# Last batch of a cross-attention and FFN kernel: gate and up on all 256 columns, roots split between VectorE and GpSimd

## The chip, the cores and the metric

The kernel runs on one core of one Trainium2 chip. The metric is device time in microseconds of one execution. A core has TensorE (PE in the profile, PEld its weight loads), VectorE (DVE), ScalarE (ACT), GpSimd (POOL) and the queue that issues transfers (SP). They run their own instruction lists and meet only at semaphores.

## The reference

`x` is (8 batches, 256 rows, 256 features), the context (8, 77, 256). All of it is float32; the FFN weights are integers scaled by 1/127.

```python
x = x + xattn(layernorm(x), ctx)         # 16 heads of 64, softmax, w_out, bias, tanh(gate)
x = x + ffn(layernorm(x))

def ffn(x):                              # HIDDEN = 768
    gate = x @ wg.T ; up = x @ wu.T
    h = silu(gate) * up
    return h @ wd.T
```

## The kernel before

After a start-up phase (weights, `t_all`, values) the kernel runs eight rounds, one per batch of 256 rows (two tiles of 128 rows, t = 0 and 1, called a and b in names). A round does the attention of batch b and, filled in between, the FFN of batch b-1. Each engine has its stages in an order written out by hand (`PE_ORDER`, `DVE_ORDER`, `ACT_ORDER`, `POOL_ORDER`). After the last attention there is nothing left to fill in, so the last batch's projection, second layernorm and FFN have orders of their own (`PE_END`, `DVE_END`, `ACT_END`, `POOL_END`): the tail, from about 288 us on. A name such as `O0.7` is stage O0 of round 7.

Float32 products are made from a high part, rounded to float32r, and a low part, the rest: ScalarE makes `_hi`, VectorE or GpSimd subtracts for `_lo`, and TensorE adds the products.

The stages of the tail:
- O0, O1 (lines 883 to 891): output projection of tile a and b, 24 matmuls each. R0, R1 (1315, 1318): the residual sum and its statistics.
- na0 to na11, nb0 to nb11 (1359 to 1382): per tile, aggregation of the statistics, variance plus eps, a seed of the inverse root and three refinements of three steps, each waiting for the one before. la, lb (1386): normalisation into `x1_hat`.
- xa, xb: on TensorE two transposes of `x1_hat` (804), on ScalarE `x2_hi` (1030), on VectorE `x2_lo` (1391). The tile on TensorE goes to banks 0 and 6 of PSUM.
- ga0 to ga5, gb0 to gb5 (844): for each of six slices f of the hidden dimension, eight matmuls of one tile: gate and up, high and low, two halves of the contraction.
- ta, tb (ScalarE, 1035): tanh of the gate. Ha, Hb (VectorE, 1399, 1402): gating and product with up. ha, hb: `h_hi` on ScalarE (1040), `h_lo` on GpSimd (1148).
- D0.7, D1.7 (870, 873): the down projection of batch 6, 12 matmuls each, put between. Y0.7, Y1.7 its results (1307). da, db (855, 857): that of the last batch, 12 matmuls each. ya, yb its results, each followed by a store of the tile (539).

In the other rounds gate and up (825) treat both tiles at once, 256 columns, eight matmuls per f. `hid_of` and `tanh_of` give the last batch a place of its own for each f, so that no slice waits for an earlier one's buffer there.

GpSimd has a routine of its own for inverse roots, used at the start for the first layernorm:

```python
        def rsqrt(step, r, v, half, tmp):
            tt = nc.gpsimd.tensor_tensor
            n = v.shape[1]
            step(tt(half, v, consts[:, 1, 0:n], ALU.mult))
            step(nc.gpsimd.tensor_scalar(r.bitcast(I32), v.bitcast(I32), -0.5, RSQRT_SEED, ALU.mult, ALU.add))
            for _ in range(3):
                step(tt(tmp, r, r, ALU.mult))
                step(tt(tmp, tmp, half, ALU.mult))
                step(tt(tmp, tmp, consts[:, 2, 0:n], ALU.add))
                step(tt(r, tmp, r, ALU.mult))
```

Of the kernel before, what the change touches and what calls it, by code (L numbers as in the profile page):

```python
# [30 lines left out]
P = 128  # L31
# [26 lines left out]
PE_END = "O0.7 O1.7 xa D0.7 ga0 ga1 ga2 ga3 ga4 ga5 xb D1.7 gb0 gb1 gb2 gb3 gb4 gb5 da db".split()  # L58
ACT_END = "xa ta0 ta1 ha0 ta2 ha1 ta3 ha2 ta4 ha3 ta5 xb ha4 tb0 ha5 tb1 hb0 tb2 hb1 tb3 hb2 tb4 hb3 tb5 hb4 hb5".split()
DVE_END = ("R0.7 na0 na1 na2 na3 na4 na5 na6 na7 na8 na9 na10 na11 la R1.7 xa nb0 nb1 nb2 Y0.7 nb3 nb4 Ha0 nb5 nb6 Ha1 nb7 nb8 Ha2 "  # L60
           "nb9 nb10 nb11 lb Ha3 Ha4 xb Ha5 Hb0 Y1.7 Hb1 Hb2 Hb3 Hb4 Hb5 ya yb").split()
POOL_END = "ha0 ha1 ha2 ha3 ha4 ha5 hb0 hb1 hb2 hb3 hb4 hb5".split()
# [16 lines left out]
def xattn_ffn_kernel(nc, x, ctx_in, ln_gamma, ln_beta, w_q, w_kv, w_out, b_out, gate,  # L79
# [26 lines left out]
    X_STEPS = 4 + 12  # L106
    assert HB * K <= BANK and DC == 2 and NT == 2 and 2 * DH == P and RC == VS + 1 and K <= P
# [7 lines left out]
    with whole:  # L115
# [138 lines left out]
        x1_done, stat_done, ln_step, x1hat_done = sem("x1_done"), sem("stat_done"), sem("ln_step"), sem("x1hat_done")  # L254
        aggr_done, spare_cleared = sem("aggr_done"), sem("spare_cleared")
# [133 lines left out]

        def count_in_tile(t, f):  # L390

            return FC * (B - 1) + FC * t + f + 1
# [214 lines left out]
        def _(pe):  # L607
# [221 lines left out]
            def gate_up_tile(t, f, general):  # L829

                if f == 0:
                    pe.wait_ge(x2hi_done, B + t)
                if t == 1:
                    pe.wait_ge(hid_done, count_in_tile(0, f))
                elif LAST_BANKS[f] == bank["D0"]:
# [12 lines left out]
            def down_tile(t, general):  # L848

                if t == 0:  # L850
                    pe.wait_ge(y_done, NT * (B - 1))
                o = ps[:, LAST_DOWN_BANKS[t], 0:D]
                for f in range(FC):
                    pe.wait_ge(hhi_done, count_in_tile(t, f))
                    mm(o, whole(h_hi[:, f, tile(t)], general), whole(wd[:, f, :], general), start=f == 0, stop=False)
                    pe.wait_ge(hlo_done, count_in_tile(t, f))
                    ins = mm(o, whole(h_lo[:, f, tile(t)], general), whole(wd[:, f, :], general), start=False, stop=f == FC - 1)
                ins.then_inc(down_done, 1)
# [34 lines left out]
            def stages_of(general):  # L893
# [11 lines left out]
                for t in range(NT):  # L905
                    stages["x" + "ab"[t]] = ("start", transpose_x1_tile, t)
                    stages["d" + "ab"[t]] = ("start", down_tile, t, general)
                    for f in range(FC):
                        stages["g" + "ab"[t] + str(f)] = ("start", gate_up_tile, t, f, general)
# [16 lines left out]
        def _(act):  # L926
# [105 lines left out]
            def tanh_tile(t, f):  # L1032

                act.wait_ge(gu_done, count_in_tile(t, f))
                nc.scalar.activation(tanh_of(B, f)[:, tile(t)], gate_up_psum(B, f)[:, tile(t)], ACT.Tanh,
                                     scale=QUANT / 2).then_inc(tanh_done, 1)

            def split_h_tile(t, f):
                act.wait_ge(hid_done, count_in_tile(t, f))
                nc.scalar.copy(h_hi[:, f, tile(t)], hid_of(B, f)[:, tile(t)]).then_inc(hhi_done, 1)  # L1040

            def tanh(b, f):

                act.wait_ge(gu_done, FC * (b - 1) + f + 1)
                if f >= 2:
                    act.wait_ge(gated, FC * (b - 1) + f - 1)
# [18 lines left out]
            for t in range(NT):  # L1065
                stages["x" + "ab"[t]] = ("start", split_x2_tile, t)
                for f in range(FC):
                    stages["t" + "ab"[t] + str(f)] = ("start", tanh_tile, t, f)
                    stages["h" + "ab"[t] + str(f)] = ("start", split_h_tile, t, f)
# [7 lines left out]
        def _(pool):  # L1077
# [62 lines left out]

            def split_h(b, f):
                pool.wait_ge(hhi_done, FC * (b - 1) + f + 1)
                nc.gpsimd.tensor_tensor(h_lo[:, f, :], hid_of(b, f), h_hi[:, f, :].bitcast(F32),  # L1143
                                        ALU.subtract).then_inc(hlo_done, 1)

            def split_h_tile(t, f):
                pool.wait_ge(hhi_done, count_in_tile(t, f))
                nc.gpsimd.tensor_tensor(h_lo[:, f, tile(t)], hid_of(B, f)[:, tile(t)], h_hi[:, f, tile(t)].bitcast(F32),
                                        ALU.subtract).then_inc(hlo_done, 1)
# [12 lines left out]
            for f in range(FC):  # L1162
                stages[f"h{f}"] = ("ffn", split_h, f)
                for t in range(NT):
                    stages["h" + "ab"[t] + str(f)] = ("start", split_h_tile, t, f)
            stages["XS"], stages["XS2"] = ("start", x_scales, 0, FIRST_X), ("first", x_scales, FIRST_X, B)
            stages["WO"] = ("first", wout_lo)
# [8 lines left out]
        def _(dve):  # L1176
# [100 lines left out]
            def hidden(b, f):  # L1277
# [3 lines left out]
                if f >= 2:  # L1281
# [77 lines left out]
            def scale_step_tile(t, i):  # L1359

                col = slice(t, t + 1)
                done = LN_STEPS * (B - 1 + t)
                if i == 0:
                    dve.wait_ge(stat_done, NT * (B - 1) + t + 1)
                    nc.vector.bn_aggr(mv[:, t, :], stats[:, t, :]).then_inc(aggr_done, 1)
                    return
                if i == 1:
                    dve.wait_ge(aggr_done, NT * (B - 1) + t + 1)
# [15 lines left out]
            def normalise_x1_tile(t):  # L1384
                dve.wait_ge(ln_step, LN_STEPS * (B + t))
# [7 lines left out]

            def hidden_tile(t, f):

                n = count_in_tile(t, f)
                h, psum = hid_of(B, f)[:, tile(t)], gate_up_psum(B, f)
                dve.wait_ge(tanh_done, n)
                nc.vector.scalar_tensor_tensor(h, tanh_of(B, f)[:, tile(t)], 1.0, psum[:, tile(t)], ALU.add,
                                               ALU.mult).then_inc(gated, 1)  # L1400
                dve.wait_ge(gated, n)
                nc.vector.tensor_tensor(h, h, psum[:, Q + t * P:Q + (t + 1) * P], ALU.mult).then_inc(hid_done, 1)
# [10 lines left out]
            for f in range(FC):  # L1413
                stages[f"H{f}"] = ("ffn", hidden, f)
            for t in range(NT):
# [4 lines left out]
                for i in range(LN_STEPS + 1):  # L1420
                    stages[f"n{name}{i}"] = ("start", scale_step_tile, t, i)
                for f in range(FC):
                    stages[f"H{name}{f}"] = ("start", hidden_tile, t, f)
# [35 lines left out]
```

## Time and profile before

| | |
|---|---|
| time, median of 3 runs | 317.37 us (316.65 to 319.08) |
| the profiled execution | 316.46 us, of which its span is 314.6 |
| TensorE busy | 298.3 us (95%), 2399 matmuls |
| VectorE, ScalarE, GpSimd busy | 235.3, 172.2 and 167.0 us |
| mean granted TensorE clock | 0.999 of full speed |

The span goes from the first to the last instruction; what lies around it makes the rest of the time. Busy shares are means over all stages. A row of the timeline gives start, duration, engine, line, operation, output from input with sizes, and in square brackets how long the engine had been idle and what it waited for. Matmuls are pipelined: each takes some 0.28 us from start to end, but the next starts long before. The trace leaves numbers out of names: `x_hat`, `x_hi` and `x_lo` are here `x1_hat`, `x2_hi` and `x2_lo`, and `x_hat` of lines 785 and 1300 the first layernorm's.

### The profile page before, as it was taken

Reading aid. Unit: us, or ns where it says so; the run is one execution under the profiler, and the core shown is the slowest. Engines: PE = TensorE matmul, PEld = TensorE weight load, DVE = VectorE, ACT = ScalarE, POOL = GpSimd, SP = SyncE. Lnnn points to the kernel's source line nnn. Section 1 sums busy time; section 2 is a strip of 40 time slices with the busy share of each in tenths; the row PEclk is TensorE's granted clock in tenths of the full one; section 3 lists DMA queues with packets and bytes.
Section 4 is the critical chain, followed back from the end, with each engine's and each line's share of the span. In section 5 each row is a group of like instructions: output and inputs, shape, how many; then the busy total and the mean of one; then the engine's idle time right before and its main releaser. Section 6 shows DMA issues by size and latency. Waiting matters only on the chain.

```text
span 314.6 us, 6453 instructions
## 1 busy us (share of the span) xinstructions
PE 298.3 (95%) x2399; PEld 275.8 (88%) x2399; DVE 235.3 (75%) x622; ACT 172.2 (55%) x338; POOL 167.0 (53%) x170
## 2 busy tenths in 40 slices
PE   7799999897987999999999999999999999989896
PEld 7798977686885999889988989898999889978896
DVE  1298887596785887878887797778787878784873
ACT  4356874658325852773486249535942772465142
POOL 2390863347853871668096629644771668045042
PEclk9999999999999999999999999999999999999999
DMA  6993153512414021102201120202020101100001
GB/s 201 387 361 84 35 205 138 174 52 102 138 55 118 2 73 35 33 3 74 68 0 32 44 69 0 76 0 69 1 77 33 35 0 43 56 13 0 2 0 70
DMA packets 16314, 23.29 MB, mean 74 GB/s; under 512 B 1634, under 2 KB 13898, under 8 KB 16282
## 3 DMA queue, kind: packets, MB, share of 16 engines
q1 hardware_dynamic: 16282, 22.85, 22.3%
q8 instruction: 21, 0.34, 0.5%
q14 instruction: 11, 0.09, 0.1%
HBM read 15.87 MB, written 4.62 MB: 65 GB/s over the span
## 4 chain that ended last, share of the span: by engine, by line
PE 80%; POOL 10%; issue 3%; DVE 2%; ACT 2%; DMA 2%; SPq 0%; POOLq 0%; ACTq 0%; DVEq 0%
PE ps L825 11%; PE ps L771 8%; PE ps L757 7%; PE ps L731 5%; PE ps L739 5%; PE ps L735 5%; PE ps L658 4%; PE ps L886 4%; PE ps L890 4%; PE ps L887 4%; PE ps L844 3%; PE ps L873 3%; PE ps L870 3%; POOL probs L1127 3%; POOL t_lo L1134 3%
## 5 line engine op out<-in xcount | busy, mean ns | idle before, releaser
L1127 POOL TENSOR_TENSOR probs<-probs,total 128x616 f32<-128x616 f32 x32 | 39.1, 1221 | 75.7 <-DVE total L1260 75.7
L978 ACT COPY pt<-ps 77x512 f32<-77x512 f32 x64 | 34.2, 584 | 49.2 <-PE ps L757 49.2
L1134 POOL TENSOR_TENSOR t_lo<-t_all,t_hi 128x1232 fp32r<-128x1232 f32 x16 | 45.6, 2849 | 4.7 <-ACT t_hi L1003 4.7
L1143 POOL TENSOR_TENSOR h_lo<-hid,h_hi 128x256 fp32r<-128x256 f32 x42 | 31.0, 737 | 28.4 <-ACT h_hi L1053 28.4
L757 PE MATMUL ps<-ident,probs 128*77 128x128 f32 x256 | 33.3, 273 | 4.3 <-POOL probs L1127 3.0
L886 PE MATMUL ps<-wo_hi,o_hi 128*128 128x256 f32 x128 | 36.3, 284 | 0.0
L887 PE MATMUL ps<-wo_lo,o_hi 128*128 128x256 f32 x128 | 36.1, 282 | 0.0
L890 PE MATMUL ps<-wo_hi,o_lo 128*128 128x256 f32 x128 | 36.0, 281 | 0.0
L1243 DVE TENSOR_REDUCE top<-ps 128x4 f32<-128x308 f32 x64 | 28.7, 472 | 9.4 <-PE ps L739 9.2
L757 PEld LDWEIGHTS ps<-ident,probs 128*77 128x77 f32 x256 | 29.5, 147 | 5.4 <-POOL probs L1127 3.7
L731 PE MATMUL ps<-t_hi,xn_hi 128*128 128x308 f32 x128 | 30.7, 321 | 0.7 <-ACT v_out L937 0.7
L771 PE MATMUL ps<-pt,v 77*64 77x256 f32 x256 | 31.2, 385 | 0.0
L991 ACT CAST o_hi<-ps 128x512 fp32r<-128x512 f32 x32 | 18.8, 587 | 21.3 <-PE ps L771 21.3
L1257 DVE TENSOR_REDUCE total<-probs 128x8 f32<-128x616 f32 x32 | 25.2, 788 | 6.5 <-ACT probs L966 6.2
L966 ACT ACTIVATE probs<-probs 128x616 f32<-128x616 f32 x32 | 22.9, 716 | 12.5 <-DVE probs L1248 12.5
L739 PE MATMUL ps<-t_hi,xn_lo 128*128 128x308 f32 x128 | 28.5, 304 | 0.0
L735 PE MATMUL ps<-t_lo,xn_hi 128*128 128x308 f32 x128 | 28.3, 302 | 0.0
L1268 DVE TENSOR_TENSOR o_lo<-ps,o_hi 128x512 fp32r<-128x512 f32 x32 | 21.3, 685 | 8.3 <-ACT o_hi L991 8.3
L1248 DVE TENSOR_TENSOR probs<-ps,top 128x308 f32<-128x308 f32 x64 | 27.3, 468 | 0.0
L1284 DVE SCALAR_TENSOR_TENSOR hid<-tanh_g,ps 128x256 f32<-128x256 f32 x42 | 17.0, 405 | 11.7 <-POOL h_lo L1143 6.4
L771 PEld LDWEIGHTS ps<-pt,v 77*64 77x64 f32 x256 | 17.0, 136 | 9.5 <-issue 1.5
L886 PEld LDWEIGHTS ps<-wo_hi,o_hi 128*128 128x128 f32 x128 | 24.0, 188 | 0.6 <-issue 0.4
(152 smaller groups left out, 819.3 us busy)
## 6 DMA issues: line engine op xcount, KB each, us to landing
v<-v_scratch SPq DMA_DIRECT2D x8, 308.0 KB
x_ln<-in_x SPq DMA_DIRECT2D x8, 256.0 KB, 4.5
v_scratch<-v_out SPq DMA_DIRECT2D x4, 512.0 KB, 2.9
stream<-in_x SPq DMA_DIRECT2D x8, 256.0 KB, 2.8
x_rooms<-in_x SPq DMA_DIRECT2D x7, 256.0 KB, 7.8
out<-stream SPq DMA_DIRECT2D x7, 256.0 KB, 2.2
wk_raw<-in_L_xattn_w_kv SPq DMA_DIRECT2D x4, 256.0 KB, 4.9
wq_raw<-in_L_xattn_w_q SPq DMA_DIRECT2D x1, 1024.0 KB, 7.7
```

The source lines that it names most:

```text
L731: mm(o, xn_hi[:, c, qs], t_hi[:, c, cols], start=c == 0, stop=False)
L735: mm(o, xn_hi[:, c, qs], t_lo[:, c, cols], start=False, stop=False)
L739: ins = mm(o, xn_lo[:, c, qs], t_hi[:, c, cols], start=False, stop=c == DC - 1)
L757: ins = nc.tensor.transpose(ps_p[0:K, m % 2, h * P:(h + 1) * P], probs[:, u, hh * K:(hh + 1) * K], ident[:])
L771: ins = mm(ps_p[e * DH:(e + 1) * DH, i, pair * Q:(pair + 1) * Q], v[:, gh * DH:(gh + 1) * DH], pt[:, h, :], start=True, stop=True)
L825: ins = mm(o[:, at:at + Q], whole(w[:, c, fs], general), whole(x2[:, c, :], general), start=x2 is x2_hi and c == 0, stop=x2 is x2_lo and c ...
L886: mm(o, o_hi[:, i, ts], wo_hi[:, i, :], start=i == 0, stop=False)
L887: mm(o, o_hi[:, i, ts], wo_lo[:, i, :], start=False, stop=False)
L890: ins = mm(o, o_lo[:, i, ts], wo_hi[:, i, :], start=False, stop=i == IC - 1)
L978: nc.scalar.copy(pt[:, q * HB:(q + 1) * HB, t * P:(t + 1) * P], ps_p[0:K, m % 2, :].rearrange("k (h q) -> k h q", h=HB)).then_inc(pt_copie ...
L1127: nc.gpsimd.tensor_tensor(p, p, total[:, u, :].unsqueeze(2).to_broadcast([P, HG, K]), ALU.mult).then_inc(probs_done, 1)
L1134: nc.gpsimd.tensor_tensor(t_lo[:, :, cols], t_all[:, :, n, cols], t_hi[:, :, cols].bitcast(F32), ALU.subtract).then_inc(tlo_done, 1)
```

## The change

Only the tail is changed.
- Gate and up of the last batch are made for both tiles in one matmul of 256 columns (`g0` to `g5`, 48 matmuls instead of 96). With them tanh, gating, product and both parts of h are on 256 columns (`t.8`, `H.8`, `h.8`, the functions of the ordinary rounds), and the last down projection `d` goes through f once, for both tiles.
- Up to the transposes the tiles stay apart. D0.7 and D1.7 run right after O1.7, ahead of both transposes.
- The inverse root of tile a is made by GpSimd (`ra`, 15 steps on one column), that of tile b by VectorE as before. `la` stands between the steps `nb5` and `nb6` of tile b.

```diff
-PE_END = "O0.7 O1.7 xa D0.7 ga0 ga1 ga2 ga3 ga4 ga5 xb D1.7 gb0 gb1 gb2 gb3 gb4 gb5 da db".split()
+PE_END = "O0.7 O1.7 D0.7 D1.7 xa xb g0 g1 g2 g3 g4 g5 d".split()
+ACT_END = "xa xb t0.8 t1.8 h0.8 t2.8 h1.8 t3.8 h2.8 t4.8 h3.8 t5.8 h4.8 h5.8".split()
+DVE_END = ("R0.7 na R1.7 nb0 nb1 nb2 nb3 nb4 nb5 la nb6 nb7 nb8 nb9 nb10 nb11 lb "
+           "Y0.7 xa xb Y1.7 H0.8 H1.8 H2.8 H3.8 H4.8 H5.8 ya yb").split()
+POOL_END = "ra h0.8 h1.8 h2.8 h3.8 h4.8 h5.8".split()
...
-            def gate_up_tile(t, f, general):
+            def last_gate_up(f, general):
                 if f == 0:
-                    pe.wait_ge(x2hi_done, B + t)
+                    pe.wait_ge(x2hi_done, B + NT - 1)
...
-                for w, at in ((wg, t * P), (wu, Q + t * P)):
+                for w, at in ((wg, 0), (wu, Q)):
                     for x2 in (x2_hi, x2_lo):
                         if f == 0 and w is wg and x2 is x2_lo:
-                            pe.wait_ge(x2lo_done, B + t)
+                            pe.wait_ge(x2lo_done, B + NT - 1)
                         for c in range(DC):
-                            ins = mm(o[:, at:at + P], whole(w[:, c, fs], general), whole(x2[:, c, tile(t)], general),
+                            ins = mm(o[:, at:at + Q], whole(w[:, c, fs], general), whole(x2[:, c, :], general),
...
+            def last_down(general):
+                pe.wait_ge(y_done, NT * (B - 1))
                 for f in range(FC):
+                    for done, h in ((hhi_done, h_hi), (hlo_done, h_lo)):
+                        pe.wait_ge(done, FC * (B - 1) + f + 1)
+                        for t in range(NT):
+                            ins = mm(ps[:, LAST_DOWN_BANKS[t], 0:D], whole(h[:, f, tile(t)], general), whole(wd[:, f, :], general),
...
+            def root_of_first_tile():
+                taken = [0]
+                def root_step(ins):
+                    taken[0] += 1
+                    ins.then_inc(first_root, 1)
+                    if taken[0] < ROOT_STEPS:
+                        pool.wait_ge(first_root, taken[0])
+                pool.wait_ge(aggr_done, NT * (B - 1) + 1)
+                col = slice(0, 1)
+                root_step(nc.gpsimd.tensor_scalar(var_eps[:, col], mv[:, col, 1], 1.0, EPS, ALU.mult, ALU.add))
+                rsqrt(root_step, rstd[:, col], var_eps[:, col], spare[:], tmp[:, col])
...
             def normalise_x1_tile(t):
-                dve.wait_ge(ln_step, LN_STEPS * (B + t))
+                if t == 0:
+                    dve.wait_ge(first_root, ROOT_STEPS)
+                else:
+                    dve.wait_ge(ln_step, LN_STEPS * B)
```

VectorE's list before, from the last step of tile a's root on: normalisation of tile a (`x1_hat`), the residual of tile b, and tile b's root behind them.

```order
L1381 SCALAR_TENSOR_TENSOR rstd<-tmp,rstd 128x1
L1386 TENSOR_SCALAR x1_hat<-stream,mv,rstd 128x256
L1315 SCALAR_TENSOR_TENSOR stream<-ps,tgate,stream 128x256
L1318 BN_STATS stats<-stream 128x6
L1391 TENSOR_TENSOR x2_lo<-ps,x2_hi 128x2x128
L1365 BN_AGGR mv<-stats 128x2
L1369 TENSOR_SCALAR var_eps<-mv 128x1
```

The same engine in the changed kernel, from tile a's aggregation to tile a's normalisation.

```order
L1355 BN_AGGR mv<-stats 128x2
L1309 SCALAR_TENSOR_TENSOR stream<-ps,tgate,stream 128x256
L1312 BN_STATS stats<-stream 128x6
L1363 BN_AGGR mv<-stats 128x2
L1367 TENSOR_SCALAR var_eps<-mv 128x1
L1371 TENSOR_SCALAR rstd<-var_eps 128x1
L1374 TENSOR_TENSOR tmp<-rstd 128x1
L1376 SCALAR_TENSOR_TENSOR tmp<-tmp,var_eps 128x1
L1379 SCALAR_TENSOR_TENSOR rstd<-tmp,rstd 128x1
L1387 TENSOR_SCALAR x1_hat<-stream,mv,rstd 128x256
```

Tile a's root steps are gone from VectorE, the residual of tile b has moved ahead of `la`, and six steps of tile b's root stand before `la`.

TensorE before, at the transposes of tile a (L804), with D0.7 and the first gate and up behind them (the end of D0.7 and the start of ga0):

```order
L870 MATMUL ps<-wd,h_hi 128x256
L873 MATMUL ps<-wd,h_lo 128x256
L844 MATMUL ps<-x2_hi,wg 128x128 x2
L844 MATMUL ps<-x2_lo,wg 128x128 x2
L844 MATMUL ps<-x2_hi,wu 128x128 x2
L844 MATMUL ps<-x2_lo,wu 128x128 x2
```

TensorE in the changed kernel, from the end of D1.7 over all four transposes to g0:

```order
L866 MATMUL ps<-wd,h_hi 128x256
L869 MATMUL ps<-wd,h_lo 128x256
L802 MATMUL ps<-ident,x1_hat 128x128 x4
L840 MATMUL ps<-x2_hi,wg 128x256 x2
L840 MATMUL ps<-x2_lo,wg 128x256 x2
L840 MATMUL ps<-x2_hi,wu 128x256 x2
L840 MATMUL ps<-x2_lo,wu 128x256 x2
```

Both down projections of batch 6 now precede the transposes, between which and gate and up nothing stands any more.

## Rows read from the trace of the kernel before

**Rows 1.** The chain of waits in order of time: start, length, engine, output, line, count.

```profile
284.15 1.90 PE ps L825 x16
...
291.03 0.50 DVE stream L1315
...
296.70 5.31 PE ps L844 x48
...
311.95 0.42 DVE stream L1307
```

**Rows 2.** The timeline of VectorE in the tail.

```profile
292.01 0.18 DVE L1365 BATCH_NORM_AGGREGATE mv<-stats 128x2 f32<-128x6 f32 x1
...
294.36 0.41 DVE L1386 TENSOR_SCALAR x_hat<-stream,mv,rstd 128x256 f32<-128x256 f32 x1
...
294.68 0.48 DVE L1315 SCALAR_TENSOR_TENSOR stream<-ps,tgate,stream 128x256 f32<-128x256 f32 x1
...
295.70 0.42 DVE L1391 TENSOR_TENSOR x_lo<-ps,x_hi 128x256 fp32r<-128x256 f32 x1
...
300.80 0.60 DVE L1386 TENSOR_SCALAR x_hat<-stream,mv,rstd 128x256 f32<-128x256 f32 x1
...
305.40 0.42 DVE L1307 SCALAR_TENSOR_TENSOR stream<-ps,stream 128x256 f32<-128x256 f32 x1
...
305.77 0.29 DVE L1399 SCALAR_TENSOR_TENSOR t_all<-t_all,ps 128x128 f32<-128x128 f32 x1
```

**Rows 3.** The timeline of TensorE and ScalarE in the tail.

```profile
293.59 0.28 PE L890 MATMUL ps<-wo_hi,o_lo 128*128 128x256 f32 x1
...
294.83 0.44 PE L804 MATMUL ps<-ident,x_hat 128*128 128x128 f32 x2 [0.96 <-DVE x_hat L1386]
...
295.30 0.37 ACT L1030 CAST x_hi<-ps 128x256 fp32r<-128x256 f32 x1 [4.80 <-PE ps L804]
...
308.83 0.33 PE L855 MATMUL ps<-wd,h_hi 128*128 128x256 f32 x1
...
311.64 0.28 PE L857 MATMUL ps<-wd,h_lo 128*128 128x256 f32 x1
```

**Rows 4.** The timeline of GpSimd's root steps at 88 us, with one step of VectorE.

```profile
87.90 0.19 POOL L1109 COPY mean<-mv 128x8 f32<-128x8 f32 x1
...
90.74 0.16 DVE L1347 SCALAR_TENSOR_TENSOR tmp<-tmp,var_eps 128x2 f32<-128x2 f32 x1
90.75 0.23 POOL L456 TENSOR_TENSOR tmp<-tmp,consts 128x8 f32<-128x8 f32 x1
...
92.17 0.20 POOL L457 TENSOR_TENSOR rstd<-tmp,rstd 128x8 f32<-128x8 f32 x1
```

**Rows 5.** The timeline of one slice of h on 256 columns, round 7.

```profile
285.01 0.42 DVE L1284 SCALAR_TENSOR_TENSOR hid<-tanh_g,ps 128x256 f32<-128x256 f32 x1 [2.07 <-POOL h_lo L1143]
...
285.13 0.39 ACT L1047 ACTIVATE tanh_g<-ps 128x256 f32<-128x256 f32 x1
...
285.47 0.42 DVE L1287 TENSOR_TENSOR hid<-hid,ps 128x256 f32<-128x256 f32 x1
...
285.92 0.41 ACT L1053 CAST h_hi<-hid 128x256 fp32r<-128x256 f32 x1 [0.41 <-DVE hid L1287]
...
286.41 0.73 POOL L1143 TENSOR_TENSOR h_lo<-hid,h_hi 128x256 fp32r<-128x256 f32 x1 [0.47 <-ACT h_hi L1053]
```

**Rows 6.** The timeline of TensorE after a wait for x2_lo.

```profile
100.00 0.50 PE L825 MATMUL ps<-x_lo,wg 128*128 128x256 f32 x2 [0.60 <-DVE x_lo L1274]
...
100.34 0.40 PE L825 MATMUL ps<-x_hi,wu 128*128 128x256 f32 x2
```

**Rows 7.** One stretch: busy us of PE, PEld, DVE, ACT, POOL, granted clock, DMA share.

```profile
74.00:76.00 2.00, 0.22 (x2) 0.16 (x2) 1.97 (x6) 1.50 (x2) 1.43 (x2) 1.00 0.00 0
```

**Rows 8.** The last two stores: one stretch as above, then their issues.

```profile
311.30:312.50 1.20, 0.62 (x6) 0.41 (x4) 0.42 (x1) 0.00 (x0) 0.00 (x0) 1.00 0.30 109
...
L539 SPq DMA_DIRECT2D out<-stream x2: 350/354/357, 311.0 to 312.4; - x2
```

More of the change, by code:

```diff
@@ L106, in xattn_ffn_kernel @@
     X_STEPS = 4 + 12
+    ROOT_STEPS = 3 + 12
     assert HB * K <= BANK and DC == 2 and NT == 2 and 2 * DH == P and RC == VS + 1 and K <= P
@@ L838, in gate_up_tile @@
                 o = gate_up_psum(B, f)
-                for w, at in ((wg, t * P), (wu, Q + t * P)):
+                for w, at in ((wg, 0), (wu, Q)):
                     for x2 in (x2_hi, x2_lo):
                         if f == 0 and w is wg and x2 is x2_lo:
-                            pe.wait_ge(x2lo_done, B + t)
+                            pe.wait_ge(x2lo_done, B + NT - 1)
                         for c in range(DC):
-                            ins = mm(o[:, at:at + P], whole(w[:, c, fs], general), whole(x2[:, c, tile(t)], general),
+                            ins = mm(o[:, at:at + Q], whole(w[:, c, fs], general), whole(x2[:, c, :], general),
                                      start=x2 is x2_hi and c == 0, stop=x2 is x2_lo and c == DC - 1)
                 ins.then_inc(gu_done, 1)
[L848 to L852, printed above, removed]
+            def last_down(general):
+                pe.wait_ge(y_done, NT * (B - 1))
                 for f in range(FC):
[L854 to L858, printed above, removed]
+                    for done, h in ((hhi_done, h_hi), (hlo_done, h_lo)):
+                        pe.wait_ge(done, FC * (B - 1) + f + 1)
+                        for t in range(NT):
+                            ins = mm(ps[:, LAST_DOWN_BANKS[t], 0:D], whole(h[:, f, tile(t)], general), whole(wd[:, f, :], general),
+                                     start=f == 0 and h is h_hi, stop=f == FC - 1 and h is h_lo)
+                            if f == FC - 1 and h is h_lo:
+                                ins.then_inc(down_done, 1)
             def down(b, t, general):
@@ L906, in stages_of @@
                     stages["x" + "ab"[t]] = ("start", transpose_x1_tile, t)
-                    stages["d" + "ab"[t]] = ("start", down_tile, t, general)
-                    for f in range(FC):
-                        stages["g" + "ab"[t] + str(f)] = ("start", gate_up_tile, t, f, general)
+                for f in range(FC):
+                    stages[f"g{f}"] = ("start", last_gate_up, f, general)
+                stages["d"] = ("start", last_down, general)
                 stages["FL"] = ("start", transpose_largest)
@@ L1030, in split_x2_tile @@
                 nc.scalar.copy(x2_hi[:, :, tile(t)], x1t_psum(t)).then_inc(x2hi_done, 1)
[L1032 to L1040, printed above, removed]
             def tanh(b, f):
                 act.wait_ge(gu_done, FC * (b - 1) + f + 1)
-                if f >= 2:
+                if f >= 2 and not last(b):
                     act.wait_ge(gated, FC * (b - 1) + f - 1)
@@ L1163, in _ @@
                 stages[f"h{f}"] = ("ffn", split_h, f)
-                for t in range(NT):
-                    stages["h" + "ab"[t] + str(f)] = ("start", split_h_tile, t, f)
             stages["XS"], stages["XS2"] = ("start", x_scales, 0, FIRST_X), ("first", x_scales, FIRST_X, B)
+            stages["ra"] = ("start", root_of_first_tile)
             stages["WO"] = ("first", wout_lo)
@@ L1280, in hidden @@
                 dve.wait_ge(tanh_done, n + 1)
-                if f >= 2:
+                if f >= 2 and not last(b):
                     dve.wait_ge(hlo_done, n - 1)
@@ L1414, in _ @@
                 stages[f"H{f}"] = ("ffn", hidden, f)
+            stages["na"] = ("start", aggregate_first)
+            for i in range(LN_STEPS + 1):
+                stages[f"nb{i}"] = ("start", scale_step_second, i)
             for t in range(NT):
@@ L1419, in _ @@
                 stages["y" + name] = ("start", result, B, t)
[L1420 to L1423, printed above, removed]
             for b in range(FIRST_X, B):
```

42 lines of the change are left out of this document (12 added, 30 removed).

## The prediction

> **What bounds the kernel now.** I read the engine table first: TensorE is busy 298.3 of 314.6 us, so time goes only where its work is shortened or where a hole in it closes. The change touches nothing before the last batch's tail, so the second view is the chain of waits from 287.9 us on [rows 1]. The reader is to see that from 291.03 to 294.8 us the chain runs through VectorE (residual, statistics, a row of tiny root steps, normalisation) while TensorE finishes O1.7 at 293.9 and then stands 0.96 us [rows 3]; and that from 294.83 on it is TensorE alone up to the last result: `xa`, D0.7, gate and up of tile a, `xb`, D1.7, gate and up of tile b, and 24 matmuls of `da` and `db` to 311.92. The tail is thus bound by TensorE's issue pace, and a matmul's price is its start-to-start distance.
>
> **Gate and up on 256 columns.** Before, each tile's gate and up is 48 matmuls on 128 columns in 5.31 us [rows 1], 0.1106 us each, twice: 10.62 us. In the ordinary rounds 16 matmuls on 256 columns take 1.90 us [rows 1], 0.1185 each. The changed kernel has 48 of these: 5.69 us. **Saved: 4.93 us.** This is the whole gain, and a wide matmul costs only 0.008 us more than a narrow one. D0.7, D1.7 and the 24 matmuls of the last down projection keep their number; the latter start from 308.83 to 311.64, 0.122 apart [rows 3].
>
> **What is given back: the chain ahead of the first gate matmul.** Before, the second tile's root (its 12 steps on VectorE are threaded between other work) and its normalisation lay under tile a's gate and up. Now g0 waits for both tiles, and that cover is gone. I follow the new order with the durations of before.
> R0.7 and `na` stay: the aggregate starts at 292.01 and ends 292.19 [rows 2].
> GpSimd's root starts about 0.08 us later (the distance from ScalarE's cast ending at 286.33 to GpSimd's 286.41 in [rows 5]): 292.27. Before shows this routine on 8 columns: from 87.90 to 92.17 there are 15 intervals, 0.285 us each, of which two were stretched by 0.02 to 0.03 [rows 4]. I take 0.282. Fifteen steps: the last starts 14 x 0.282 = 3.95 later, 296.22, and ends 296.42; `la` can start at 296.50.
> VectorE meanwhile: R1.7 no longer stands behind `la`. The last matmul of O1.7 starts at 293.59 [rows 3]; a result follows the last matmul's start by 0.31 (311.64 to 311.95, [rows 1, 3]), so R1.7 starts at 293.90 and `nb0` 0.98 later as in R0.7 to `na` (291.03 to 292.01, [rows 1, 2]): 294.88. From there the steps go at 0.196 (twelve intervals from 292.01 to 294.36, [rows 2]): `nb5` starts at 295.86 and ends at 296.02, 0.16 long [rows 4]. `la` therefore waits for GpSimd about 0.45 us, and that is on the path.
> Then: `la` 296.50; next step 0.32 later (294.36 to 294.68, [rows 2]): 296.82; six steps of 0.196: `lb` at 298.00. Transposes 0.47 after it (294.36 to 294.83, [rows 2, 3]): 298.47; ScalarE's x2_hi 0.47 on (294.83 to 295.30, [rows 3]): 298.94; VectorE's x2_lo 0.40 on (to 295.70, [rows 2]): 299.34; the first matmul that needs x2_lo 0.46 on (its 0.42 plus 0.04): 299.80. Y0.7 and `xa` lie between `lb` and `xb` on VectorE at 298.31 and 298.68 and end at 299.10, ahead of 299.34, so they cost nothing; if they were 0.25 later, they would delay `xb`. Only two matmuls of g0 are done by then.
> On TensorE D0.7 and D1.7 now follow O1.7 at once: 24 x 0.12 from 293.71 to 296.6, under the roots. What remains idle there is some 0.3 us before `xa`, 1.1 before `xb`, 0.4 before g0 and 0.2 inside it. These holes, 2.0 us against 0.96, plus the transposes that no longer hide, are the price.
> The other 46 matmuls: the first pair after such a wait takes 0.34 instead of 0.24 ([rows 6], 100.00 to 100.34), so the last starts at 299.80 + 0.10 + 45 x 0.1185 = **305.23**.
>
> **The last down projection.** In TensorE's stream it would run at 0.12 from 305.35, with f5's h_lo wanted at 307.99. The chain of f5 on 256 columns gives: tanh 0.31 after the last matmul's start, 305.54; then 0.42 (ScalarE's 0.39 plus 0.03), 305.96; then 0.46, 0.45, 0.49 as in [rows 5] (gating to product, to cast, to GpSimd), subtraction at 307.36, plus 0.73 and 0.05: 308.14. So the chain is last by 0.15 us, matmuls of f5's h_lo start at 308.14 (tile a) and 308.26 (tile b). Before that the four engines keep up: per f, TensorE needs 0.95 us, VectorE 0.46 + 0.42, ScalarE 0.39 + 0.41, GpSimd 0.73 plus 0.08 [rows 5].
> The two tiles now end together: `ya` at 308.45 and `yb` behind it on VectorE by 0.37 (305.40 to 305.77, [rows 2]) at **308.82**. Before it started at 311.95: 3.13 us earlier. The two stores are issued 0.37 instead of 1.4 us apart; an issue takes 0.35 [rows 8], as long as that distance. Their transfers may meet; no row shows two so close, so it costs between 0 and 0.4 us (one transfer kept the DMA engines busy for 0.30 x 1.20 = 0.36, [rows 8]). I take 0.1, since an issue spaces them as far as that.
> **Sum:** 3.13 - 0.1 = **3.0 us**. The profiled execution took 316.46 us in all (span 314.6), so 313.4 for its like. It lies 0.9 below the median 317.37; the four times shown have their middle at 317.0, from which I get **314.0 us**, 1.1% under the median. No change would be told from noise within about 1%, so this stands at the edge.
>
> **Unknown costs and bounds.** GpSimd on one column is not in the trace. Nearest row: 8 columns, 0.28 apart; A step of VectorE takes 0.16 on two columns [rows 4] and no less on one, since the steps follow at 0.196 there too [rows 2]. Lower end 0.26 apart: `la` 0.3 earlier. Upper end 0.31, every step stretched as [rows 4] shows once: `la` 0.4 later. Bounds of the whole gain with the stores: 2.2 to 3.6 us.
>
> **Rivals.** *The two engines hold each other up.* In [rows 4] VectorE's tiny steps run beside the root on GpSimd, which is stretched by at most 0.03 a step; but `la` itself took 0.60 instead of 0.41 when it began together with GpSimd's h_lo at 300.80 [rows 2], so holding up exists. As a mechanism here: while GpSimd makes the root, VectorE runs five steps (`nb1` to `nb5`) of 0.16. If each held a step of GpSimd for its full length, `la` would come 0.8 later: gain 2.2, 314.8 us. Against it stand the sixteen steps of [rows 4]. Chance 0.13. The Trainium skill ("SBUF — State Buffer", Who interferes with whom) says that a VectorE instruction with two SBUF inputs or in a 2-port mode and a GpSimd instruction that reads SBUF share one port pair, and that the second fully blocks until the first is done. By that rule the gain would be the smaller one; the row of `la` agrees with it, the rows of the root show far less than it allows.
> *The tail of f5 is the bound.* If one engine of the hidden chain falls behind 0.95 us per f (GpSimd and VectorE are at 0.81 and 0.88), the lag grows over six f; 0.1 per f costs 0.6 us: 314.6 us. For it: ScalarE has tanh and cast in one queue, t5 ahead of h4. Against: the sums above. Chance 0.09.
> *Root not late.* If GpSimd is faster on one column and the stores don't meet, the gain is 3.6 to 3.9: 313.3 us. Chance 0.12.
> *Slower: the matmul clock falls in the holes.* TensorE is to stand about 2.0 of the 3.4 us before 299.8. If its granted clock fell to the lower of its two levels, 1.2 of 2.4 GHz, each of the 70 matmuls left would take up to 0.12 more; it decides from 25 of them on (3.0 / 0.12), and all 70 give 8.4 - 3.0 = 5.4 us slower, 322 us. Against: from 74 to 76 us TensorE was busy 0.22 of 2.00 and the granted clock was 1.00 in that stretch [rows 7], as in every other of 2 us up to the end. Chance 0.02.
> *The change does nothing*, because the end hangs on something else, such as the stores: the chain of waits goes from TensorE to the last result without a gap [rows 1]. Chance 0.01, 317 us.
>
> **How the numbers follow.** My forecast has the other 0.63. From its own bounds (gain 2.5 to 3.5) and the scatter of single medians (316.65 to 317.37 for most) a bit over half of it lies below 314.2, the mark of 1%: 0.63 x 0.6 = 0.38, plus all of the root not late, 0.12, plus a few hundredths of the two smaller gains: faster 0.53. Slower by over 1% only by the clock: 0.02, and I add 0.01. The rest, 0.44, is within 1%. The range runs from the larger gain and a low median (312.9) to the rivals with gains of 2.2 and a high one (315.3).
>
> **What would show each step.** Gate and up of the last batch: one group of 48 matmuls on 128x256, 0.118 to 0.120 us apart. GpSimd: 15 steps from about 292.3 to 296.4, and VectorE waiting some 0.45 us for them before `la`. TensorE waiting about 1.1 us for x1_hat before `xb` and 0.2 us for x2_lo within g0. The last gate matmul near 305.2, `yb` at 308.8. I am wrong if the root ends after 297.2, if TensorE waits for h_lo in the last down projection by more than 0.3, or if the time from `yb` to the end grows beyond the 2.65 us of before.

## The result and the profile after

| | before | changed |
|---|---|---|
| median | 317.21 us (19 executions, 316.00 to 319.51) | 315.46 us (19, 313.96 to 316.64) |
| profiled execution | 316.46 us, span 314.6 | 314.06 us, span 312.1 |
| TensorE busy | 298.3 us, 2399 matmuls | 293.8 us, 2351 matmuls |

The ratio is 0.9949 with an interval of 0.9932 to 0.9966: the changed kernel is 0.5% faster, 1.75 us, where 3.0 was forecast, and 315.46 us lies just above the range.

I compare the profiled executions first, both at a mean granted clock of 0.999 or 1.0. The chain of waits of the changed kernel (columns as in [rows 1]):

```profile
291.15 0.50 DVE stream L1309
...
292.13 0.19 DVE mv L1355
...
292.40 0.20 POOL var_eps L1137
...
296.21 0.20 POOL rstd L455
...
296.44 0.41 DVE x_hat L1387
...
297.93 0.42 DVE x_hat L1387
...
298.40 0.45 PE ps L802 x2
...
299.30 6.20 PE ps L840 x48
305.50 2.60 PE ps L851 x22
...
308.13 0.40 PE ps L851
...
308.56 0.42 DVE stream L1301
```

It answers to [rows 1]. From 291 to 299.3 us the chain is that of the two roots; from there to 308.5 it is TensorE again. All of gate and up now takes one piece of 6.20 us, its wait for x2_lo included, where one tile alone took 5.31.

VectorE's timeline around the normalisations and at the end (columns as in [rows 2]):

```profile
295.99 0.16 DVE L1379 SCALAR_TENSOR_TENSOR rstd<-tmp,rstd 128x1 f32<-128x1 f32 x1
296.44 0.41 DVE L1387 TENSOR_SCALAR x_hat<-stream,mv,rstd 128x256 f32<-128x256 f32 x1 [0.29 <-POOL rstd L455]
...
308.56 0.76 DVE L1301 SCALAR_TENSOR_TENSOR stream<-ps,stream 128x256 f32<-128x256 f32 x2 [1.73 <-PE ps L851]
```

`la` waits 0.29 us for GpSimd's root and takes its usual 0.41. The last row holds `ya` and `yb`, 0.34 apart (0.76 less 0.42), so `yb` starts at 308.90.

TensorE's timeline, from the last matmul of O1.7 to the first of g0 that needs x2_lo; it answers to [rows 3]:

```profile
293.71 0.28 PE L886 MATMUL ps<-wo_hi,o_lo 128*128 128x256 f32 x1
...
296.56 0.28 PE L869 MATMUL ps<-wd,h_lo 128*128 128x256 f32 x1
296.91 0.44 PE L802 MATMUL ps<-ident,x_hat 128*128 128x128 f32 x2
298.40 0.44 PE L802 MATMUL ps<-ident,x_hat 128*128 128x128 f32 x2 [1.05 <-DVE x_hat L1387]
299.30 0.50 PE L840 MATMUL ps<-x_hi,wg 128*128 128x256 f32 x2 [0.46 <-ACT x_hi L1026]
299.76 0.39 PE L840 MATMUL ps<-x_lo,wg 128*128 128x256 f32 x1
```

The last store issues, answering to [rows 8]:

```profile
309.01 1.15 SPq L537 DMA_DIRECT2D out<-stream  x2
```

Two issues of 0.35 us fill 1.15, so the second begins 0.80 behind the first, at 309.8. Tile b's result began at 308.90, and tile a's store was issued 0.45 after its result began; by that distance tile b's could have gone at 309.35. The span ends at 312.1, 3.20 us behind `yb`, where before it was 2.65.

### The profile page after: what moved, and what is told of

Read it like the earlier page. It is cut to its first block, busy times and chain, and to the rows that moved or that the text cites. A ratio compares the mean times of both kernels' runs of the same rounds, so it can differ in the third digit from the quotient of the medians.

```text
span 312.1 us, 6330 instructions
## 1 busy us (share of the span) xinstructions
PE 293.8 (94%) x2351; PEld 270.1 (87%) x2351; DVE 232.0 (74%) x599; ACT 171.3 (55%) x326; POOL 168.9 (54%) x179
## 4 chain that ended last, share of the span: by engine, by line
PE 78%; POOL 11%; issue 3%; ACT 3%; DVE 2%; DMA 2%; SPq 0%; DVEq 0%; POOLq 0%
PE ps L823 11%; PE ps L769 8%; PE ps L755 7%; PE ps L729 5%; PE ps L737 5%; PE ps L733 5%; PE ps L656 4%; PE ps L882 4%; PE ps L886 4%; PE ps L883 4%; PE ps L866 3%; PE ps L869 3%; POOL probs L1110 3%; POOL t_lo L1117 3%; PE ps L840 2%
```

## Experiments

Executions of one kernel differ in their mean granted clock: 1.00, about 0.994 or about 0.989. "At full clock" means 0.998 or more. I read about 0.994 as one fall of the clock and about 0.989 (everything below 0.992) as two: the four profiles at 0.992 to 0.995 have one, at 100 us, and the one at 0.989 has two. The other executions have their mean only. Every ratio is against the kernel before, measured beside it on the same chip.

**The changed kernel and the kernel before, again.** No edit.

> The changed kernel once more, unedited. Its 19 timed executions ran at mean granted clocks of 1.0 down to 0.988, and the two at 1.0 took 314.0 us where the median is 315.5. Theory C (the clock falls in the tail's holes in most executions): some executions at 0.989 to 0.995 again, longer by about 1.4 us at 0.994 and 2.5 at 0.989; if the profiled one is such a one, the granted clock by stretch is 1.00 up to about 299 us and under 1 only behind it, where the matmuls of gate and up then go at up to 0.22 us. Theory N (it falls at any place of the program and the change has nothing to do with it): the low clock lies in earlier rounds as well, and the kernel before shows the same means.

> The kernel before as the one measured, so that its clocks are seen execution by execution. Theory C: mean granted clock 0.998 or more in nearly all, times 316.0 to 317.5. Theory N: 0.989 to 0.995 in most of them, as in the changed kernel, so that the clock explains none of the missing gain.

Measured: changed 315.64 us, ratio 0.9974 (0.9954 to 0.9994); before 317.3 us, ratio 1.0004 (0.9986 to 1.0022). The unedited kernel stays within its own noise, so half a per cent can be told. The profiles of both show something that neither of the first two profiles has. Here the kernel before, in stretches of 2 us (columns as in [rows 7]):

```profile
98.00:100.00 2.00, 0.89 (x6) 0.69 (x6) 1.96 (x5) 0.69 (x3) 0.24 (x1) 1.00 0.03 8
100.00:102.00 2.00, 1.71 (x8) 1.71 (x9) 2.00 (x6) 1.28 (x4) 2.00 (x2) 0.62 0.00 0
102.00:104.00 2.00, 2.00 (x12) 2.00 (x11) 1.72 (x4) 0.68 (x3) 2.00 (x2) 0.53 0.00 0
104.00:106.00 2.00, 2.00 (x20) 2.00 (x19) 1.36 (x4) 1.83 (x5) 1.54 (x2) 1.00 0.00 0
```

The granted clock falls to the lower level (0.50, 1.2 GHz) for some 3.5 us, just behind a stretch in which TensorE was busy 0.89 of 2.00. The next question was whether the changed tail, with its holes, does that too.

**Unread matmuls in the holes.** The edit puts 9 matmuls whose result nobody reads between the transposes, and 4 ahead of g0:

```diff
-PE_END = "O0.7 O1.7 D0.7 D1.7 xa xb g0 g1 g2 g3 g4 g5 d".split()
+PE_END = "O0.7 O1.7 D0.7 D1.7 xa w9 xb w4 g0 g1 g2 g3 g4 g5 d".split()
+            def keep_busy(times):
+                for _ in range(times):
+                    mm(ps[:, 5, 0:D], o_hi[:, 0, 0:P], wo_hi[:, 0, :], start=True, stop=True)
```

> The changed kernel with matmuls that nobody reads in two of the holes of TensorE: 9 between the transposes of tile a and tile b (a hole of 1.05 us) and 4 ahead of g0 (0.46 us), 0.12 us each. Theory C: the clock stays at 1.0 in nearly all executions, and the median falls to 314.0 to 314.4, the ratio to 0.990 to 0.991. Theory N: nothing changes, median 315.5, clocks 0.988 to 1.0. If the fillers are too many, the first gate matmul comes later by 0.1 us or so.

Measured: 315.01 us, ratio 0.9945 (0.9921 to 0.9969). TensorE's timeline of this kernel:

```profile
299.18 0.44 PE L802 MATMUL ps<-ident,x_hat 128*128 128x128 f32 x2
299.37 1.32 PE L830 MATMUL ps<-wo_hi,o_hi 128*128 128x256 f32 x9
300.67 0.44 PE L802 MATMUL ps<-ident,x_hat 128*128 128x128 f32 x2
300.86 0.71 PE L830 MATMUL ps<-wo_hi,o_hi 128*128 128x256 f32 x4
301.57 0.50 PE L845 MATMUL ps<-x_hi,wg 128*128 128x256 f32 x2
```

`xa` to `xb` is 1.49 us and `xb` to g0 0.90, as without them (296.91, 298.40, 299.30): the unread matmuls cost no time on the path. One execution of 12 was below 0.992 (at 0.986), against 3 of 12 of the unedited kernel on the same chip; its median is 0.6 us lower. That points the right way, but the intervals overlap, and the 314.0 to 314.4 us of the expectation were missed: eight of the 12 were below full clock. The profile, at 0.992, has its fall at 100 us (0.50 from 102 to 104) and 1.00 all through the tail.

**Both roots in one chain on VectorE**, on two columns, with `la` and `lb` behind it, and nothing on GpSimd:

```diff
-DVE_END = ("R0.7 na R1.7 nb0 nb1 nb2 nb3 nb4 nb5 la nb6 nb7 nb8 nb9 nb10 nb11 lb "
+DVE_END = ("R0.7 na R1.7 nb0 nb1 nb2 nb3 nb4 nb5 nb6 nb7 nb8 nb9 nb10 nb11 la lb "
-POOL_END = "ra h0.8 h1.8 h2.8 h3.8 h4.8 h5.8".split()
+POOL_END = "h0.8 h1.8 h2.8 h3.8 h4.8 h5.8".split()
-                col = slice(1, 2)
+                col = slice(0, 2)
```

> The root of tile a is taken from GpSimd: VectorE makes both roots in one chain of steps on two columns after the second tile's statistics, then la and lb. In the profile of the changed kernel la starts at 296.44, lb at 297.93. Here the eleven steps follow the aggregate at 295.00 in 0.195 each, so la at 297.34 and lb at 297.67, transposes of tile b 0.26 earlier. Theory (the root on GpSimd is on the path and costs more than it saves): the last result 0.1 to 0.3 us earlier at the same clock. Rival: ScalarE's and VectorE's splits of the two tiles now collide (xa's x2_lo before xb's), and the last result is 0.0 to 0.3 later. The hole of TensorE after D1.7 becomes one of 1.1 us ahead of both transposes; by theory C its clock falls no less often than in the changed kernel.

Measured: 314.75 us, ratio 0.9944 (0.9924 to 0.9964); profiled 313.88 us, span 312.1. Its chain of waits:

```profile
297.25 0.42 DVE x_hat L1384
...
297.72 0.45 PE ps L802 x2
...
298.94 0.86 PE ps L840 x3
...
308.21 0.42 DVE stream L1301
```

The first result comes at 308.21, 0.35 earlier than with GpSimd's help; 0.14 of that is a head start (O1.7's last matmul at 293.57 instead of 293.71), 0.21 the chain. The span is no shorter, since from there to the end it took 3.89 us instead of 3.54; both stores again stand on SP's queue.

**The last store on ScalarE's queue.**

```diff
-                    for t in range(NT):
-                        sp.wait_ge(y_done, NT * (b - 1) + t + 1)
-                        sp.dma_start(out_dram[:, b - 1, t], residual_of(b, 1)[:, t]).then_inc(y_out, 16)
+                    sp.wait_ge(y_done, NT * (b - 1) + 1)
+                    sp.dma_start(out_dram[:, b - 1, 0], residual_of(b, 1)[:, 0]).then_inc(y_out, 16)
...
+            act.wait_ge(y_done, NT * B)
+            nc.scalar.dma_start(out_dram[:, B - 1, 1], residual_of(B, 1)[:, 1]).then_inc(y_out, 16)
```

> The changed kernel with the store of the last tile issued from ScalarE's queue instead of the one that has just issued the first tile's. In the changed kernel's profile the two issues start 0.80 us apart although the results are 0.33 apart; in the kernel before nothing was queued. Theory (the issue queue is taken for 0.80 us per store): the second store starts within 0.1 of yb's end and lands 0.3 to 0.5 us earlier, and the median falls by as much, to 315.0 to 315.2. Rival (the two transfers share the DMA engines, or the landing is what costs): the end moves by under 0.15. The holes of TensorE are those of the changed kernel, so a profile with a mean clock of 0.989 shows, by theory C, clocks of 0.5 at 100 to 104 and again behind 299.

Measured: 315.98 us, ratio 0.9963 (0.9931 to 0.9996); profiled 316.02, span 313.9. The two issues in its timeline:

```profile
311.07 0.36 SPq L536 DMA_DIRECT2D out<-stream  x1
...
311.41 0.37 ACTq L1058 DMA_DIRECT2D out<-stream  x1
```

They are 0.34 us apart instead of 0.80, and from the first result (310.62) to the end it takes 3.28. The other profiles bear this out. Eight kernels have both last stores on SP's queue and their two results 0.34 apart; from the first result to the end they take 3.53 to 3.89 us, 3.69 on average. Four have the second store on ScalarE's queue: 3.06 to 3.28, 3.19 on average. The ranges do not overlap; the second queue is worth **0.50 us**. The Trainium skill ("DMA: Bandwidth & Descriptors", Issuing engines are not separate DMA queues) says that a second issuing engine saves only the time of initiating a transfer; the runs agree: the issues came 0.46 us closer, and the end 0.50.

The median is no lower all the same, and the same profile shows why: four of its six executions were at 0.989. The expected 315.0 to 315.2 us were missed. Up to its last matmul this kernel has the TensorE stream of the changed kernel. Its stretches:

```profile
100.00:102.00 2.00, 2.00 (x11) 2.00 (x11) 2.00 (x5) 0.92 (x2) 2.00 (x2) 0.50 0.00 0
...
298.00:300.00 2.00, 0.58 (x3) 0.35 (x4) 1.62 (x7) 0.69 (x2) 0.00 (x0) 1.00 0.00 0
300.00:302.00 2.00, 2.00 (x13) 1.84 (x14) 0.84 (x3) 0.38 (x1) 0.00 (x0) 0.80 0.21 79
302.00:304.00 2.00, 2.00 (x11) 2.00 (x11) 1.14 (x4) 0.68 (x2) 0.24 (x1) 0.50 0.14 52
304.00:306.00 2.00, 2.00 (x17) 2.00 (x16) 1.13 (x3) 0.98 (x3) 1.03 (x2) 0.84 0.00 0
```

Here is the second fall: behind the tail's holes, while gate and up is running. The same stretches of the changed kernel's first profile:

```profile
300.00:302.00 2.00, 2.00 (x19) 2.00 (x18) 0.81 (x3) 0.66 (x2) 0.00 (x0) 1.00 0.36 131
302.00:304.00 2.00, 2.00 (x19) 2.00 (x18) 1.75 (x5) 1.67 (x5) 1.20 (x2) 1.00 0.00 0
```

11 matmuls in a stretch against 19. The chain of waits gives the price:

```profile
299.85 7.71 PE ps L839 x48
...
310.62 0.42 DVE stream L1302
```

Gate and up takes 7.71 us instead of 6.20: **1.51 us** for one fall in the tail. It starts 0.55 later than in the changed kernel's first profile (299.30), and this execution has a fall at 100 us that the other has not. It is the only profile with wide matmuls that shows a fall in the tail. The changed kernel profiled again stood as long in front of gate and up (busy 0.56 of 2.00 from 298 to 300 us) and kept 1.00 behind it.

**The holes filled at both places.** The unread matmuls of before, and 10 more ahead of the transposes of the first layernorm in the round at 100 us:

```diff
+                if isinstance(n, int) and n == 2:
+                    claim(n - 1, "XT")
+                    for _ in range(10):
+                        mm(ps[:, bank["XT"], 0:D], wo_hi[:, 0, 0:P], wo_hi[:, 0, :], start=True, stop=True)
```

> The changed kernel with the 9 and 4 unread matmuls in the tail's holes and 10 more ahead of the transposes of the first layernorm in round 1, in the hole at 97.3 to 98.5 us (idle 1.25 us), after which two profiles showed the granted clock at 0.50 from 100 to 103.5. Theory C2 (two places where TensorE stands, each followed by a fall of the clock in part of the executions, the one at 100 us in both kernels, the one in the tail in the changed kernel alone): with both filled nearly all executions have a mean clock of 0.998 or more and the median is 314.0 to 314.3, ratio 0.990 to 0.992. If only the tail matters: median 315.0 as with the tail's fillers alone. Rival: the clock falls for a reason that has nothing to do with holes; then the share of executions at 0.994 stays at a half or more.

Measured: 317.47 us, ratio 0.9981 (0.9932 to 1.003): not to be told from the kernel before. The six go from 313.62 and 314.71 at full clock to 318.41, wider apart than one clock fall explains. The expected 314.0 to 314.3 us did not come. Three of six were at about 0.994, as if the matmuls at 100 us had not removed the first fall; none of the three was profiled, and in the next kernel, with the same matmuls there, it is one of six. What they do is not shown. Its profiled execution, 316.98 us at 0.999, is one of the long ones, and in it TensorE stands 2.42 us at 63.96 us. The next kernel shows the same pause.

**All of it at once**: the joint root, ScalarE's queue, 8 and 5 unread matmuls in the tail, 10 at 100 us.

> All that the experiments point to: both roots in one chain on VectorE, the last store on ScalarE's queue, 8 unread matmuls ahead of the transposes, 5 ahead of g0 and 10 at 97 us. Sum by the theories: 314.06 at full clock for the changed kernel, less 0.2 for the joined roots, less 0.4 for the store: 313.4 us, in nearly all executions at a mean clock of 0.998 or more, ratio 0.988 to 0.990. If the store gives nothing: 313.9.

Measured: 315.94 us (313.26 to 317.62), ratio 0.9955 (0.9913 to 0.9998), five of six at full clock, where 313.4 us was expected. So a full clock alone does not give the short time. Its profile is a long one, 316.02 us, and TensorE's timeline has:

```profile
63.68 0.45 PE L736 MATMUL ps<-t_hi,xn_lo 128*128 128x308 f32 x2
66.54 0.66 PE L754 MATMUL ps<-ident,probs 128*77 128x128 f32 x4 [2.42 <-issue]
```

TensorE stands 2.42 us with nothing that it waits for. The place is around the start of the loop over rounds. The profile of the previous kernel has a pause of the same length at the same place, that of the first kernel with unread matmuls one of 1.09 us, and that of the next kernel, which has no unread matmuls, one of 1.67. They lie far ahead of the tail; they are a third source of scatter. What makes them was not tried.

**Is it the clock?** The strong test is a kernel whose tail matmuls are narrow: gate and up as 96 matmuls of 128 columns, with all else as in the changed kernel.

```diff
-                for w, at in ((wg, 0), (wu, Q)):
+                for w, at, t in ((wg, 0, 0), (wg, P, 1), (wu, Q, 0), (wu, Q + P, 1)):
...
-                            ins = mm(o[:, at:at + Q], whole(w[:, c, fs], general), whole(x2[:, c, :], general),
+                            ins = mm(o[:, at:at + P], whole(w[:, c, fs], general), whole(x2[:, c, tile(t)], general),
```

> The changed kernel, but gate and up of the last batch as 96 matmuls on 128 columns (each f still one stage, all other engines on 256 columns). By the prediction's term 96 x 0.1106 - 48 x 0.1185 = 4.93 us more: last result near 313.5 in the profile, median 320.4. Rival (wide and narrow cost more alike than the rows say, or the last stage is bound by another engine): less than 4 us more.

Measured: 330.53 us, ratio 1.0427 (1.0397 to 1.0457), 15 us above the changed kernel where the width alone, from [rows 1], is worth 4.9. All six executions were at 0.957 to 0.964. Its stretches:

```profile
298.00:300.00 2.00, 0.77 (x4) 0.50 (x4) 1.65 (x7) 0.51 (x2) 0.00 (x0) 1.00 0.00 0
300.00:302.00 2.00, 1.98 (x11) 1.87 (x10) 0.41 (x2) 0.00 (x0) 0.00 (x0) 0.57 0.31 111
...
320.00:322.00 2.00, 2.00 (x11) 2.00 (x11) 0.84 (x2) 0.96 (x3) 0.73 (x1) 0.50 0.00 0
...
324.00:326.00 2.00, 1.00 (x8) 0.80 (x7) 0.76 (x2) 0.00 (x0) 0.00 (x0) 0.96 0.00 0
```

And its chain of waits:

```profile
300.13 20.22 PE ps L840 x94
320.36 4.54 PE ps L851 x23
```

Behind the same holes the clock falls and stays down through all of gate and up, with TensorE busy all the time. It comes back only at about 324 us, some 4 us into the last down projection, whose matmuls are 256 columns wide.

**Narrow, with the holes filled** by 9 and 4 unread matmuls, the two edits above together.

> The kernel with 96 narrow gate and up matmuls, plus the 9 and 4 unread matmuls in the tail's holes. Without them it took 330.5 us: its clock fell to 0.50 at 300 us in all six executions and stayed there. Theory C (the holes ahead of gate and up make the clock fall; narrow matmuls alone do not raise it again): with the holes filled the clock stays up, and what is left of the 15 us is the term for width, 4.9 us: 314.1 + 4.9 = 319.0 at full clock, mean clock 0.994 to 1.0. Rival (narrow matmuls themselves bring it down here): again 329 to 331 us at 0.96.

Measured: 319.56 us, ratio 1.0087 (1.0062 to 1.0112), 11.0 us less than the same kernel without them. Its stretches, and then its chain of waits:

```profile
298.00:300.00 2.00, 2.00 (x15) 1.59 (x13) 1.66 (x7) 0.49 (x2) 0.00 (x0) 1.00 0.00 0
300.00:302.00 2.00, 1.98 (x18) 1.88 (x17) 0.40 (x2) 0.06 (x1) 0.00 (x0) 1.00 0.31 114
```

```profile
299.68 0.42 PE ps L845 x2
...
300.12 10.71 PE ps L845 x94
310.83 3.04 PE ps L856 x23
...
313.89 0.42 DVE stream L1307
```

Gate and up takes 10.71 us instead of 20.22, the down projection 3.04 instead of 4.54: together 11.0 us, as much as the medians differ by. This settles the mechanism for narrow matmuls: matmuls that do no work the kernel needs, put into the holes, keep the clock up, and narrow ones behind them do not bring it down. Why the clock fell in all six executions there, and in a share of them with wide matmuls, is not shown. The pair also measures the width at full clock: from the first gate matmul to the first result 14.21 us (299.68 to 313.89) against 9.26 (299.30 to 308.56) in the changed kernel, 4.95 us. The forecast had 4.93.

**The best pieces, with and without unread matmuls.** Joint root and ScalarE's queue, in one kernel with 8 and 5 unread matmuls in the tail, in the other with none; and **the down projection spread** over the holes, in the changed kernel:

```diff
-PE_END = "O0.7 O1.7 D0.7 D1.7 xa xb g0 g1 g2 g3 g4 g5 d".split()
+PE_END = "O0.7 O1.7 D0.7 xa D1.7 xb g0 g1 g2 g3 g4 g5 d".split()
```

> Both roots in one chain on VectorE, the last store on ScalarE's queue, 8 unread matmuls ahead of the transposes and 5 ahead of g0; nothing at 97 us. At full clock 314.06 - 0.2 - 0.5 = 313.4 us. Theory C: mean clocks of 0.998 or more in about half of the executions (as the kernel before, which falls only at 100 us) and hardly any at 0.991 or less; median 313.9 to 314.3. Rival: as many low ones as the next kernel.

> The same without the unread matmuls. At full clock the same 313.4 us. Theory C: the clock falls in the tail in some two thirds of the executions, so mean clocks at 0.991 or less in a quarter or more, and the median 1.0 us above that of the kernel with them, 314.9 to 315.3. Rival: no difference between the two.

> The changed kernel with D1.7 between the transposes of tile a and of tile b instead of ahead of both: real work in the hole of 1.05 us, while the hole ahead of tile a's transposes grows from 0.2 to 1.65 us. The last result comes 0.2 us later by D1.7's end (12 x 0.12 after 297.15). Theory C says that what counts is how long TensorE stands altogether in a stretch, which stays the same: clock as in the changed kernel, median 315.5 to 315.9. Rival: the hole right before gate and up counts, which is now 0.46 alone: full clock in half of the executions and the median under 315.0.

| | median | ratio | at full clock, about 0.994, about 0.989 |
|---|---|---|---|
| joint, ScalarE's queue, filled | 313.87 us | 0.9925 (0.9895 to 0.9954) | 3, 3, 0 |
| joint, ScalarE's queue | 313.76 us | 0.9915 (0.9891 to 0.9939) | 2, 3, 1 |
| spread | 314.81 us | 0.9941 (0.9922 to 0.9961) | 3, 1, 2 |

Either of the first two is 0.8% faster than the kernel before; their medians are 1.6 to 1.7 us under the changed kernel's 315.46, but on another chip. But the two are alike: the difference of 1.0 us that the clock should have made between them was not seen. On this chip the unfilled kernel had one execution of six at 0.989; in so few, a fall that comes in a share of executions is easily missed. The spread kernel has its g0 at 299.72 in the profile, 0.42 later than the changed one. Its low executions are at 0.991, 0.991 and 0.992, so that its classes are less clear than the others'. What came is the rival of its expectation (under 315.0 us, half of the executions at full clock) and not the 315.5 to 315.9 of its theory; six executions do not prove the rival.

Over all executions with a clock on record: of 56 executions of the five kernels with wide matmuls and an unfilled tail (the changed one, joint, ScalarE's queue alone, both, spread), 17 were at about 0.989 and 10 at full clock; of 30 with a filled tail 1 and 15; of 63 of the kernel before 2 and 30 (one execution of 748 us is left out). If each fall comes by itself, a fall at 100 us comes in about half of the executions whatever the tail is, and a second one, in the tail, in some six in ten where the holes are open (no fall at all in 10 of 56, 0.18, is 0.5 x 0.36; both in 17 of 56, 0.30, is 0.5 x 0.6), and hardly ever where they are filled.

## Why the prediction was off

**Right: the path.** Up to the results every step came within 0.13 us of its forecast. Two small things cancel in this, which is luck: the stages ahead ended 0.12 late (O1.7's last matmul at 293.71, before at 293.59), and GpSimd's root took 0.14 less than forecast. GpSimd's root began at 292.40 (forecast 292.27) and took 14 distances in 3.81 us, 0.272 each (3.95, 0.282); `la` 296.44 (296.50), `lb` 297.93 (298.00), the second transposes 298.40 (298.47), first x2_lo matmul 299.76 (299.80), first matmul of f5's h_lo 308.13 (308.14), `yb` 308.90 (308.82). The hidden chain kept up: TensorE's matmuls of f5's h_lo come 0.19 us late, where 0.15 was forecast. TensorE stood 1.58 us between 296 and 300 us (busy 1.28 and 1.14 of 2.00 in its two stretches), where holes of 2.0 were forecast. The width term of 4.93 us measured 4.95.

**Right: engines do not hold each other up here.** GpSimd's steps took 0.19 to 0.20 us and followed at 0.27 beside VectorE's as they did while VectorE stood, and `la` took 0.41. The rival that gave each overlap its full length, 0.8 us later, has nothing for it in these rows. The joint root shows that the helper was not needed at all: one chain on two columns is 0.21 us earlier. I had not weighed that, since it is no part of the change.

**Wrong, first: "I take 0.1, since an issue spaces them as far as that."** The stores' term was mis-sized. The last of the prediction's own signs of being wrong, the time from `yb` to the end, is the one that came true. Its working rested on [rows 8], an issue of 0.35 us, and took an issue's length for the distance at which the next can follow. On SP the second begins 0.80 behind the first. From `yb` to the end it took 3.20 us, 0.55 more than before, where 0.1 was taken and 0.4 was the upper bound. Over the eight profiles with both stores on SP it is 3.35 on average (3.69 less 0.34), 0.70 more than before; the four with two queues have the issues closer (0.34 apart in the one shown) and take 0.50 of it back. What the remaining 0.2 is, the transfers meeting or something else, was not separated.

**Wrong, second and larger in the miss: "Slower: the matmul clock falls in the holes ... Chance 0.02."** The mechanism happens, in a form that the rival did not have. I priced it as all or nothing, 70 matmuls at the lower level for 5.4 us net loss, and gave it 0.02 because of the row of [rows 7], where the clock stood at 1.00 with TensorE busy 0.22 of 2.00. What the runs show is a fall in a share of the executions, of some 3.5 us, costing 1.51. A single profile that had no fall could not speak against that; the kernel before, profiled again, has one at 100 us. The narrow kernel shows that a form near the full one exists too: down for 24 us, 11.0 us lost. A matmul at the lower level cost 0.095 more (0.213 against 0.118), where up to 0.12 was taken.

**The sum.** The forecast for a profiled execution at full clock was 313.4 us, and it took 314.06: of the 0.66, 0.45 are the stores, 0.08 the path up to `yb` (308.90 for 308.82), 0.10 what lies around the span (1.96 us where it was 1.86), the rest rounding. From there to the median I took some 0.6 for both kernels alike. (The bounds that the chances were worked out from, a gain of 2.5 to 3.5, are also narrower than the 2.2 to 3.6 stated for the whole gain.) For the kernel before it is 317.21 - 316.51 (its 30 executions at full clock) = 0.70, but for the changed one 315.46 - 314.06 (three at full clock) = 1.40; its executions have a second fall to meet. This 0.8 beyond the 0.6 is the larger part of the 1.46 by which the median missed its forecast. At equal, full clock the change is worth 316.51 - 314.06 = 2.45 us; the clock takes 0.70 of that from the median, and 1.75 is left. The 0.70 is an accounting over executions; that holes cause the fall is shown by the narrow pair, while for the wide tail itself the medians with and without unread matmuls differed in one comparison by 0.6 us, within the noise, and in the other not at all. What supports it there is the count of executions at about 0.989 (17 of 56 against 1 of 30) and the one profile with a fall in the tail.

**Open:** how much the holes cost the wide kernel in the median, what sets in which executions the clock falls, what the pauses of TensorE at the start of the loop come from, and whether the transfers of the two last stores delay each other.

## What to carry to other kernels

Price a change of order in the executions as they are, not in one profile: ask of each new hole on TensorE whether the clock may fall behind it in some executions, and compare the kernels both at equal clock and in the median. Where TensorE must wait in a tail, unread matmuls in the hole cost nothing on the path and can keep the clock: with narrow matmuls behind the hole they were worth 11.0 us here, with wide ones less than these runs can tell. When two small transfers end a kernel together, give them two queues (0.50 us here), and before two engines share a chain of tiny steps, try both columns in one chain.

## What the runs showed of the hardware

- Behind a hole, TensorE's granted clock fell to 0.50 while it was busy again, and came back with matmuls of 256 columns after some 3.5 us (301 to 304.5 us above), but not in 20 us of back-to-back matmuls of 128 columns; there it came back some 4 us after matmuls of 256 columns had taken over (at about 324 us). At the lower level both widths were about 0.213 us apart (two of either kind take 0.63 from start to end); at full clock 0.118 and 0.114.
- Two stores issued back to back on SP's queue began 0.80 us apart, though each issue takes 0.35; on two queues they began 0.34 apart, and the kernels ended 0.50 us earlier on average.
- A step of GpSimd on one column took 0.19 to 0.20 us and followed at 0.272, hardly less than on 8 columns (0.285, [rows 4]); VectorE's followed at 0.19 to 0.20 on one column or two.
- TensorE paused 1.09 to 2.42 us around the start of the loop over rounds with nothing to wait for, at full clock, in four of the 14 profiles.
